# Second phase: maxima of the scores thirteen steps ahead of the scores instead of fourteen

## The reference, cut to what matters

```
s1 = einsum('bshe,bthe->bhst', q1, k1) / scale      # q1, k1: per-head projections
s2 = einsum('bshe,bthe->bhst', q2, k2) / scale      # a second pair of projections
attn = softmax(s1, axis=-1) - gain * softmax(s2, axis=-1)
o = einsum('bhst,bthe->bshe', attn, vp)
o = (o - mean(o)) / sqrt(var(o) + EPS)              # per head
out = o.reshape(B, S, D) @ wo.T
```

## Time and profile before

| | |
|---|---|
| median of three runs | 1512.58 us |
| profiled execution | 1511.9 us, its span 1510.1 us |
| PE busy | 1472.2 us (97%) |
| DVE busy | 1145.5 us (76%) |
| ACT busy | 847.0 us (56%) |
| GpSimd busy | 381.6 us (25%) |
| chain that ended last | PE 82%, DVE 8%, SP queue 3%, ACT 3% |
| granted TensorE clock | 0.999 on average |

### The profile page before, as it was taken

The page is one execution under the profiler, slowest core; times in us unless marked ns, Lnnn a source line. Parts: engine busy times, 40 slices in busy tenths (PEclk is TensorE's granted clock), DMA queues, the critical chain, the costliest instruction groups (busy, mean ns, idle before and its releaser), DMA issues.

```text
span 1510.1 us, 28696 instructions
## 1 busy us (share of the span) xinstructions
PE 1472.2 (97%) x11021; PEld 1042.9 (69%) x11021; DVE 1145.5 (76%) x2315; ACT 847.0 (56%) x1123; POOL 381.6 (25%) x410
## 2 busy tenths in 40 slices
PE   9999999999999999999999999999999999999998
PEld 5333343435566666666656888898989898998987
DVE  6445544468999999999967898878787878778786
ACT  5888899976788888888874331222222231222221
POOL 1000000133646667666452420000000000000001
PEclk9999999999999999999999999999999999999999
DMA  7756656456655656656652201100010101100001
GB/s 153 145 110 120 111 111 125 88 106 110 96 92 97 96 97 101 106 83 95 99 176 71 75 17 29 25 20 28 19 38 15 36 22 29 26 22 25 20 24 28
DMA packets 89887, 108.91 MB, mean 72 GB/s; under 512 B 18244, under 2 KB 58192, under 8 KB 89752
## 3 DMA queue, kind: packets, MB, share of 16 engines
q1 hardware_dynamic: 89624, 106.90, 37.5%
q10 hardware_dynamic: 128, 0.20, 0.0%
HBM read 26.29 MB, written 4.19 MB: 20 GB/s over the span
## 4 chain that ended last, share of the span: by engine, by line
PE 82%; DVE 8%; SPq 3%; ACT 3%; issue 2%; DMA 1%; POOL 0%; POOLq 0%; DVEq 0%; ACTq 0%
PE ps L109 78%; SPq L119 3%; DVE NM L1609 2%; PE ps L1385 2%; ACT PX L1553 1%; ACT H L683 1%; DMA R_ml_w<-in_ml_w_dram 1%; PE ps L1393 1%; PE ps L1347 1%; DVE EE L850 1%; PE ps L1316 0%; DVE QS L757 0%; DVE GH L2476 0%; DVE X L931 0%; DMA WS<-SM 0%
## 5 line engine op out<-in xcount | busy, mean ns | idle before, releaser
L1609 DVE TENSOR_REDUCE NM<-ps 128x4 f32<-128x1024 f32 x256 | 307.3, 1220 | 25.6 <-PE ps L109 25.2
L1553 ACT ACTIVATE PX<-ps 128x1024 f32<-128x1024 f32 x256 | 262.4, 1025 | 79.4 <-PE ps L109 77.5
L683 ACT ACTIVATE H<-ps,b1c 128x1024 f32<-128x1024 f32 x256 | 267.7, 1119 | 38.3 <-PE ps L109 36.9
L2247 ACT ACTIVATE GF<-ps,cols 128x512 f32<-128x512 f32 x128 | 87.2, 688 | 219.2 <-PE ps L109 200.8
L109 PE MATMUL ps<-XC,W_sw_w 128*128 128x512 f32 x768 | 187.1, 393 | 0.0
L109 PEld LDWEIGHTS ps<-XC,W_sw_w 128*128 128x128 f32 x768 | 140.1, 188 | 27.5
L2595 POOL TENSOR_SCALAR RSc<-AGc 128x4 f32<-128x4 f32 x23 | 6.1, 263 | 576.6 <-DVE AGc L2362 576.6
L2242 ACT ACTIVATE GF<-ps 128x512 f32<-128x512 f32 x64 | 38.2, 596 | 184.7 <-PE ps L109 184.7
L2478 DVE TENSOR_TENSOR GH<-GF,GH 128x512 fp32r<-128x512 f32 x192 | 133.2, 694 | 6.6
L109 PE MATMUL ps<-PX,VT 128*32 128x256 f32 x2048 | 137.1, 385 | 0.1
L109 PE MATMUL ps<-KT,QT 48*128 48x512 f32 x512 | 127.5, 495 | 3.1 <-DVE NM L1609 2.0
(11 more groups left out here) (253 smaller groups left out, 2506.3 us busy)
## 6 DMA issues: line engine op xcount, KB each, us to landing
KT<-KS SPq DMA_DIRECT2D x128, 192.0 KB, 4.7
ST<-QS SPq DMA_DIRECT2D x254, 96.0 KB, 2.8
QT<-XSb SPq DMA_DIRECT2D x128, 96.0 KB, 4.2
XR<-TT SPq DMA_DIRECT2D x352, 32.0 KB, 1.9
XT<-in_xT_dram SPq DMA_DIRECT2D x8, 512.0 KB, 4.1
raw_a<-in_x_dram SPq DMA_DIRECT2D x8, 512.0 KB, 4.3
CR<-in_ctxT_dram SPq DMA_DIRECT2D x8, 512.0 KB, 6.2
out_dram<-X SPq DMA_DIRECT2D x7, 512.0 KB, 2.9
```

What stands on the lines that cost most here:

```text
L683: e.activation(H1[s % 8][:, :, :], PP[s % 3][:, :, :], ACT.Tanh, bias=b1c[:, half:half + 1], scale=1.0).then_inc(act_th, 1)
L1553: e.activation(PX[s % 3][:, :, :, :], PP[2][:, :, :].rearrange("p g (c q) -> p g c q", c=2), ACT.Exp, bias=0.0, scale=0.25).then_inc(act_e ...
L1609: e.tensor_reduce(NM[u % 2][:, qc, :, :, i], PP[qc][:, :, :].rearrange("p g (m k) -> p g m k", m=2), AX.X, ALU.max, negate=True).then_inc( ...
L2247: e.activation(g[:, :], o, f, bias=cols[:, col:col + 1], scale=1.0).then_inc(act_g, 1)
```

## The change

One constant: maxima are made 13 steps ahead of the scores they belong to, and no longer 14. `rows(u)` and everything else stay in their steps.

```
@@ -980,7 +980,7 @@
-LEAD = 14
+LEAD = 13
 NU = 4 * NP
```

## The result

The changed kernel takes 1530.2 us (median of four runs, 1528.3 to 1531.3) against 1512.69 us (1510.52 to 1513.13) for the kernel before in the same session: a ratio of 1.0128, 95% interval 1.0116 to 1.0139. By the two medians it is 17.5 us slower; the ratio comes from all runs and is not the quotient of the medians (which would be 1.0116), and by it the loss is about 19 us. The profiled execution took 1530.49 us, its span is 1528.7 us; against the 1511.9 us and 1510.1 us of before that is 18.6 us. The forecast was 1531.

The account below looks back on a forecast made before the run. PE, busy for 97% of the span, was taken as the bound. Units 6 to 30 (9.5 + 5.7), first units (3) and last unit (0.7) sum to 18.9 us on 1511.9, so 1531 us; forecast 1524 to 1538, range 1517 to 1542.

Parts of the forecast that it names:

- A: Units whose number leaves 2 when divided by 4: L1347 0.40 us later, plus 0.3 us beside GpSimd's L1747.
- B: Units whose number leaves 3 when divided by 4: L1347 0.41 us later, plus 0.6 us beside GpSimd's L1709.
- C: Units whose number leaves 0 when divided by 4: L1347 0.35 us later, nothing for GpSimd.
- D: Units whose number leaves 1 when divided by 4: L1347 0.36 us later, nothing for GpSimd.
- The room: The split ended 2.2 us ahead of L1347; the change spends this and PE waits, 9.5 us over units 6 to 30.
- The lock: Units 6 to 30: DVE's split at its new time is held by GpSimd's work, 5.7 us, ends 0 and 11.4.
- The first units: Units 0 to 5: a lagging DVE delays L1347, gross 5.0 us; part returns, 3 taken, between -1.5 and 5.
- Does it stay?: Behind L1347: neither ACT nor DVE makes up the time, so all 9.5 us count; third phase only shifted.
- Absorbed: Rival: some other wait of PE shrinks by what L1347 loses, 1512.6 us within 3; 9%.
- faster: Rival: at the lagging start reductions come sooner and the MEMSET's hold goes, 2.9 us, so 1509.7; 7%.
- The lock decides: Rival: each of the 13 meetings of DVE with GpSimd costs in full, 1539.4 us, up to 1545; 14%.
- Half returns: Rival: PE's wait at L1347 is there but half returns, or reductions start earlier, 1517 to 1524 us; 12%.

Follow-up runs that it names:

- 0.9 us more room: Changed kernel (LEAD 13) with PE making the three products of `prep_k` ahead of the transposes instead of behind them: 1521.64 us, 1.0075 against the kernel before.
- second execution: The changed kernel once more, unaltered, in another session: 1536.6 us (one run).
- the kernel with the wait taken out: Changed kernel (LEAD 13), but the transposes read the split of the unit before, which is ready: 1517.7 us, 1.0044 against the kernel before.
- the context pieces moved as well: Changed kernel with transposes reading the unit before's split and GpSimd's L1709 two steps later: 1515.72 us, 1.003 against the kernel before.

## Why the prediction was right, step by step

| term | predicted | measured at L1347 |
|---|---|---|
| units 6 to 30 | 9.5 + 5.7 = 15.2 | 14.9 |
| of them 7 of A | 0.40 + 0.3 each, 4.9 | 4.65 (0.70 in the steady ones) |
| 6 of B | 0.41 + 0.6 each, 6.1 | 6.7 (1.48 four times, 0.36 twice) |
| 6 of C | 0.35 each, 2.1 | 2.3 (0.43) |
| 6 of D | 0.36 each, 2.2 | 1.3 (0.24) |
| units 0 to 5 | 3 | 4.6 |
| last unit | 0.7 | 0.5 |
| behind it | 0 | -1.4 |
| sum | 18.9 | 18.6 |

The measured ones come from these rows of the profile after, with 416.35, 764.48 and 778.38 for the same units before: lateness 4.57 at unit 5, 19.46 at unit 30, 19.99 at unit 31.

```profile
420.92 0.40 PE L1347 MATMUL ps<-C,NS 128*32 128x128 f32 x2 [1.72 <-DVE NS L1617]
...
783.94 0.39 PE L1347 MATMUL ps<-C,NS 128*32 128x128 f32 x2 [0.56 <-DVE NS L1617]
...
798.37 0.39 PE L1347 MATMUL ps<-C,NS 128*32 128x128 f32 x2 [1.10 <-DVE NS L1617]
```

- **The room.** Right. The 2.2 us were spent and 0.25 to 0.5 us more; the split moved alone repeats it, and 0.9 us more room takes it away. The room alone was priced at 0.35 in C and 0.36 in D and cost 0.24 in both (0.43 in C less the 0.19 by which its L1615 was held).
- **The lock.** Right in kind and nearly right as a sum, by a middle that no single unit shows. In A L1617 is held for 0.49 instead of 0.19 us beside L1747: the 0.3 that was taken. In B it is all or nothing. L1709 and L1617 come within 0.01 us of each other; in unit 15 GpSimd is first and DVE waits in full, in unit 23 both start at 684.96 and DVE goes through:

```profile
684.96 1.34 POOL L1709 TENSOR_TENSOR CH<-CR,CH 128x512 fp32r<-128x512 f32 x1
684.96 0.19 DVE L1617 TENSOR_TENSOR NS<-NM,NS 128x32 fp32r<-128x32 f32 x1
```

  In the second execution GpSimd was first in unit 23 too. In unit 27 no L1709 stands there. In C the cast L1615 met the end of L1709 (0.37 instead of 0.18 us), where I saw nothing that would hold it. The trace before had it: by the prediction's own numbers L1615 would start at 569.55 + 1.25 = 570.80, and L1709 ran until 571.00:

```profile
569.72 1.28 POOL L1709 TENSOR_TENSOR CH<-CR,CH 128x512 fp32r<-128x512 f32 x1
```

  That C came out near its price is luck: two errors of opposite sign.
- **The first units.** The mechanism was right and the size too small, 4.6 for 3. In unit 3 L1615 takes 0.18 us as written, and the unit catches up 0.41 where 0.3 late was the gross price. Unit 0, costed at nothing because PE waited for reductions there, waits 1.07 us for the split. Missing was the clock: units 0 and 1 cost 1.8 us in the first profile, 1.6 of them by the fall at 344, and 0.25 in the second execution, which stands at 3.26 us in unit 5.
- **Does it stay?** Nearly. 1.4 us of the 20.0 come back behind the phase, most of it at one wait of the third phase, for NTl (2.9 us before, 1.9 after), where PE arrives 19.9 us later and NTl comes only 18.9 us later. I had said "only shifted".
- **Absorbed, faster:** struck out by the 22.1 us of waits and by the units' distances. **The lock decides:** not at full price, since in A it holds one half of the split for 0.3 us; but the kernel with the wait taken out shows the path it would have taken, DVE late for L1627. **Half returns:** 7% returned.

The total came out closer than its parts deserve: 1.6 too little at the start and 1.4 too much at the end cancel. That part of the nearness is luck.

## What to carry to other kernels

A wait that is not in the trace has a room, and the room can be read off: the producer's end and the consumer's start in the same unit. A change that spends more than the room costs the difference in every unit, and from there on each further step costs at least in full (17.5 us, then 89).

When an instruction is moved, list both the new neighbours that may hold it and those that now stand behind it. The first is worth 1.1 us a time here; the second, for one addition that frees a PSUM bank, 27 us of waits in a kernel that lost 50. And look at the start of a phase on its own, since a longer lead has to be built up there.

## What the runs showed of the hardware that I had not expected

**The clock fell behind some short waits.** The changed kernel has three stretches of about 3.4 us at half the clock (1.2 GHz instead of 2.4) in the second phase, where the kernel before has none. The second of them, in windows of the profile after:

```profile
400.00:405.50 5.50, 4.09 (x40) 2.64 (x40) 5.16 (x13) 3.94 (x7) 4.84 (x7) 0.99 0.77 104
405.50:409.00 3.50, 3.50 (x28) 1.78 (x26) 2.49 (x5) 1.94 (x3) 1.83 (x3) 0.53 0.44 61
409.00:414.00 5.00, 5.00 (x52) 3.56 (x48) 4.96 (x9) 4.63 (x8) 0.00 (x0) 1.00 0.90 127
```

PE had waited 1.41 us at L1347 (until 404.22) before it fell. The others came behind waits of 1.07 and 1.72 us. But waits of 1.48 us in four units of kind B, with PE busy on either side, were followed by no fall, and the second execution went from 340 to 419 us without one, past a wait of 2.52 us. So these rows price a fall (1.6 us for the one at 344) and don't tell when one comes; that stays open. With fourteen steps, and with thirteen and the wait taken out, none of the early falls appears (in the latter although unit 0 waits 1.08 us); with the context pieces moved as well, one stands at 343.6.

**Not every GpSimd instruction holds DVE.** When they start first, casts and subtractions on 128x512 elements (L1709, L1747, L1749) and the MEMSET hold the split until they end or nearly so, and L1756 on 128x256 held the cast too (0.50 us in unit 5). L1764, a power on 128x16 elements that takes 2.93 us, doesn't: with fifteen steps the whole split runs inside it.

```profile
547.01 2.93 POOL L1764 TENSOR_TENSOR VR<-VR,nhalf 128x16 f32<-128x16 f32 x1
547.77 0.18 DVE L1615 CAST NS<-NM 128x32 fp32r<-128x32 f32 x1
547.99 0.19 DVE L1617 TENSOR_TENSOR NS<-NM,NS 128x32 fp32r<-128x32 f32 x1
```

The rule that the prediction drew on (the Trainium skill, SBUF — State Buffer, Who interferes with whom) says that whoever comes first holds the shared ports for its whole instruction, and that a DVE instruction with two SBUF inputs meets any GpSimd one that reads SBUF. The tie in kind B agrees with it (1.30 us against 0.19). Of the two places where the prediction saw it agree, its part on two inputs covers only L2298; L1615 has one input, and the MEMSET beside it reads nothing. L1764 does not agree: it reads SBUF and ran for 2.93 us, and L1617, with its two inputs in SBUF, took 0.19 us within it, in 29 units of the kernel with fifteen steps. In kind D of the changed kernel L1775, a power on 128x4 elements (596.83, 1.04 us), spares the split in the same way, and beside L1780 on 128x256 (783.29, 1.22 us) L1617 took 0.35 us, neither free nor held to the end. The ends of GpSimd's work are rough in a profile. Whether its kind or its few elements spare DVE was not tried.
